# First attention layer of a gated cross-attention model: probabilities made with keys on the partitions, row maxima added in PSUM by selector products

## The chip, the cores and the metric

One core of a Trainium2 chip runs the whole model in one launch. The engines named here are PE (TensorE), DVE (VectorE), ACT (ScalarE), POOL (GpSimd) and SP (SyncE). The metric is the device time of the launch in microseconds.

## What is computed

A batch of 32 sequences of 128 tokens of width 128 goes through four layers, each an attention to a context and a feed-forward part. Only the first attention, A0, is changed:

```python
x = x + tanh(g_xattn[0]) * L0_xattn(layernorm(x), ctx, Wq, bq, Wk, bk, Wv, bv, Wo, bo)
# 16 heads of width 8; the 16 query heads attend to 4 key and value groups
# whose sum enters (the einsums run over g)
# q = x @ Wq + bq, k = ctx @ Wk + bk, v = ctx @ Wv + bv
weight = jnp.einsum('bhtd,bgvd->bhtv', q, k) / math.sqrt(D_HEAD)
weight = jax.nn.softmax(weight, axis=-1)
out = jnp.einsum('bhtv,bgvd->bhtd', weight, v)
out = out.transpose(0, 2, 1, 3).reshape(b, t, N_HIDDEN)
return out @ Wo + bo
```

The kernel sums the four key groups into one key and one value of width 8 that all 16 heads share (`wkvs0`, `bkv0`).

## The kernel before

The kernel has eight stages, one after another: A0, F0, A1, F1, A2, F2, A3, F3. A stage starts when the last residual of the one before has been added. Within a stage the 32 sequences go in eight blocks `c` of four. In A0 two blocks are unrolled in a loop (blocks 1 to 4), the others are written out. Each engine has its own program in a fixed order, and semaphores named `A0_...` join them; so the order that is written is the order that runs.

A block of A0 has 16 rounds `u`. A round handles one unit: one sequence `j` and four of its heads, 128 queries by 4 x 128 keys, one PSUM bank. The fp32 queries and keys are split in three bf16 parts each, so that one bf16 product gives an exact score. The path of a unit before the change:

- PE, line 771: two products, queries on the partitions, into bank 0 or 1.
- DVE, `less_max` (lines 1664 and 1665): row maxima by a reduction, then the scores less the maxima, from PSUM to `ex` in SBUF.
- ACT, line 1241: exponential, SBUF to SBUF.
- PE, line 780: four fp32 transposes into bank 2 or 3, two rounds behind. ACT, line 1239: copy to `pT0`.
- Once per sequence: PE multiplies `v0` by `pT0` (line 794; a column of ones in `v0` gives the sums), ACT copies it, PE transposes it back (806), DVE divides by the sums (1745, 1746), PE transposes (810), ACT copies, PE applies `wo0` (817).
- Once per block: DVE adds the residual (1782, 1783).

Between the rounds lie pieces of the next block, in `SLICES0`: the normalised input is transposed (739), keys and values (743) and queries (747) are projected, POOL splits them into parts (`split`, lines 543 to 551 for keys and 554 to 558 for queries; the call `power` in line 529 is the inverse deviation), and PE transposes the parts (751, 757). All pieces use bank 6, so each waits until ACT has emptied the one before. DVE makes the statistics (1752, 1757, 1645) and the normalised input (1766) of two blocks ahead in `front`.

## Time and profile before

| | us |
|---|---|
| median of 3 runs | 1875.44 (1872.81 to 1878.2) |
| the profiled execution, own time | 1858.33 |
| span in its profile | 1856.5 |
| PE busy | 1383.9 |
| DVE busy | 1350.7 |
| ACT busy | 1006.0 |
| POOL busy | 491.3 |

Busy time is the time in which an engine runs instructions; it says nothing of which wait counts in a stage. The views are read by stage. "PEclk" is the granted clock of TensorE as a share of full speed. In a timeline a row gives start, duration and instruction; instructions in a row overlap at their ends, so the distance between two starts is what one costs.

### The profile page before, as it was taken

How to read it: one execution, taken by the hardware profiler on the slowest of the kernel's cores; microseconds unless marked ns; L12 is line 12 of the kernel's file. 1: busy time of each engine (PE TensorE's matmuls, PEld its weight loads, DVE VectorE, ACT ScalarE, POOL GpSimd, SP SyncE). 2: the span in 40 equal slices, each digit the busy share in tenths (PEclk: the TensorE clock that was granted, in tenths of full speed). 3: DMA queues.
4: the chain of work that ended last, by engine and by line, in shares of the span. 5: the costliest groups of instructions: out<-in, count | busy, mean ns of one | idle time of the engine just before them, and what ended most of it. 6: DMA issues, size and time to landing. Idle time of an engine off the chain costs nothing.

```text
span 1856.5 us, 35646 instructions
## 1 busy us (share of the span) xinstructions
PE 1383.9 (75%) x9716; PEld 1034.4 (56%) x9716; DVE 1350.7 (73%) x4216; ACT 1006.0 (54%) x2812; POOL 491.3 (26%) x499
## 2 busy tenths in 40 slices
PE   3677776987744446677669999999997419999990
PEld 3455553665533334533325666666666319999990
DVE  3888886788879896889955677676767456666657
ACT  3678786342324554410127776777786207777760
POOL 5433530211100000100000022342233335555550
PEclk9899988999865556978879999999999759999995
DMA  7000059400099920100000000000000422222216
GB/s 164 11 7 6 12 79 161 51 0 1 29 133 160 161 34 14 32 1 0 1 0 7 7 23 18 22 30 21 13 22 24 170 91 63 64 67 66 65 52 226
DMA packets 144708, 97.72 MB, mean 53 GB/s; under 512 B 21657, under 2 KB 133933, under 8 KB 143442
## 3 DMA queue, kind: packets, MB, share of 16 engines
q1 hardware_dynamic: 135890, 79.49, 23.2%
q0 software_dynamic: 8704, 16.87, 2.7%
q8 instruction: 53, 0.87, 0.2%
q14 instruction: 61, 0.50, 0.1%
HBM read 42.43 MB, written 54.93 MB: 52 GB/s over the span
## 4 chain that ended last, share of the span: by engine, by line
PE 35%; issue 30%; DVE 19%; ACT 9%; POOL 4%; DMA 1%; DVEq 1%; SPq 0%; ACTq 0%; POOLq 0%
PE bank L1216 6%; PE bank L1208 6%; PE bank L852 5%; ACT att L1362 3%; PE bank L868 3%; PE bank L901 3%; ACT arena L1239 2%; DVE x L2307 2%; PE bank L888 2%; POOL dispatched_rows L628 2%; PE bank L878 2%; DVE nm L1664 2%; PE bank L856 2%; DVE arena L1808 1%; DVE tmp L1942 1%
## 5 line engine op out<-in xcount | busy, mean ns | idle before, releaser
L1239 ACT ACTIVATE arena<-bank 128x512 f32<-128x512 f32 (+6 forms) x440 | 256.2, 614 | 143.2 <-PE bank L1072 62.1
L529 POOL TENSOR_TENSOR rstd<-ve,mhalf 128x4 f32<-128x4 f32 x64 | 67.0, 1046 | 686.9 <-DVE ve L1645 686.9
L1362 ACT ACTIVATE att<-bank,arena 128x128 f32<-128x128 f32 x512 | 181.9, 377 | 80.8 <-DVE arena L1808 79.0
L1582 ACT ACTIVATE att<-bank,arena 128x128 f32<-128x128 f32 x576 | 165.1, 372 | 73.1 <-PE bank L1208 72.9
L628 POOL DMA_INDIRECT dispatched_rows<-arena x128 | 132.9, 1038 | 209.9 <-DVE arena L1726 152.8
L679 POOL DMA_INDIRECT expert_outputs<-arena x144 | 143.4, 996 | 147.5 <-DVE arena L2284 133.7
L1239 ACT ACTIVATE xnT<-bank 128x128 f32<-128x128 f32 (+1 forms) x180 | 63.6, 354 | 188.8 <-PE bank L700 133.6
L1216 PE MATMUL bank<-arena,att 128*128 128x128 f32 x1152 | 154.1, 277 | 1.7 <-ACT att L1582 0.5
L1208 PE MATMUL bank<-xnT,arena 128*128 128x128 f32 x1152 | 154.1, 277 | 0.2 <-ACT xnT L1239 0.2
L1216 PEld LDWEIGHTS bank<-arena,att 128*128 128x128 f32 x1152 | 141.0, 193 | 3.8 <-ACT att L1582 3.8
L1208 PEld LDWEIGHTS bank<-xnT,arena 128*128 128x128 f32 x1152 | 141.8, 194 | 0.6 <-ACT xnT L1239 0.6
L1664 DVE TENSOR_REDUCE nm<-bank 128x4 f32<-128x512 f32 x136 | 93.2, 685 | 54.7 <-PE bank L771 53.2
L1808 DVE TENSOR_REDUCE arena<-bank 128x4 f32<-128x512 f32 x128 | 82.3, 685 | 62.5 <-PE bank L868 60.0
L2270 DVE COPY arena<-arena 128x512 f32 x144 | 61.7, 428 | 83.6 <-issue 83.5
L1241 ACT ACTIVATE att<-att 128x512 f32<-128x512 f32 x144 | 91.1, 632 | 55.8 <-DVE att L1665 49.7
L1362 ACT ACTIVATION_READ_ACCUMULATOR att<-bank,arena 128x1 f32 x512 | 110.6, 216 | 0.0
L1665 DVE TENSOR_TENSOR att<-bank,nm 128x512 f32<-128x512 f32 x136 | 94.0, 691 | 4.7
L1347 ACT ACTIVATE arena<-bank 128x512 f32<-128x512 f32 x128 | 77.7, 607 | 30.5 <-PE bank L852 30.5
L1814 DVE TENSOR_TENSOR att<-att,arena 128x512 f32<-128x512 f32 x128 | 88.7, 693 | 4.4
L868 PEld LDWEIGHTS bank<-arena 64*128 64x128 f32 x1024 | 63.1, 189 | 45.6 <-issue 24.7
L780 PE MATMUL bank<-ident,att 128*128 128x128 f32 x512 | 82.9, 287 | 2.3 <-ACT att L1241 2.1
L868 PE MATMUL bank<-arena 64*128 64x128 f32 x1024 | 75.3, 287 | 12.2 <-ACTq L1354 6.3
(314 smaller groups left out, 3256.7 us busy)
## 6 DMA issues: line engine op xcount, KB each, us to landing
dispatched_rows<-padf SPq DMA_DIRECT2D x16, 2128.5 KB, 35.3
arena<-dispatched_rows SPq DMA_DIRECT2D x144, 64.5 KB
cxT<-in_ctx SPq DMA_DIRECT2D x32, 256.0 KB, 2.9
arena<-in_L_ffn_w SPq DMA_DIRECT2D x8, 1024.0 KB, 13.1
arena<-expert_outputs SPq DMA_DIRECT2D x8, 1024.0 KB, 13.7
expert_outputs<-arena POOLq DMA_INDIRECT x144
dispatched_rows<-arena POOLq DMA_INDIRECT x128
out_x<-x SPq DMA_DIRECT2D x8, 256.0 KB, 3.1
```

The costliest lines, as they stand in the source:

```text
L628: pl.indirect_dma_start(sent, bass.IndirectOffsetOnAxis(di3[:, q:q + 1], 0), rows3[:, q, :], None)\
L679: pl.indirect_dma_start(sent_out, bass.IndirectOffsetOnAxis(xtu3[:, s, P:P + 1], 0), yt3[:, s, :], None, bounds_check=TOP3 * TOKENS - 1, o ...
L852: last = nc.tensor.matmul(A[:, :], wqk3[:, t, pair * P:pair * P + P], cxT[:, p, :] if t else xnT[:, :], start=True, stop=True)
L868: last = nc.tensor.matmul(bank[side][:, i * P:i * P + P], q, k, start=True, stop=True)
L1208: last = nc.tensor.matmul(bank[s % 2][:, k * P:k * P + P], w1c3[:, s % 4, k * P:k * P + P], xnT[:, (s % 4) * P:(s % 4) * P + P], start=Tru ...
L1216: last = nc.tensor.matmul(bank[2 + s % 2][:, 0:P], h3[:, s % 2, k * P:k * P + P], w2c3[:, s % 4, k * P:k * P + P], start=(k == 0), stop=(k ...
L1239: copy = lambda o, i: nc.scalar.activation(o, i, ACT.Copy)
L1362: last = nc.scalar.activation(ex3_of(w, side)[:, i, :], bank[side][:, i * P:i * P + P], ACT.Exp, bias=nm3[:, w % 2, h:h + 1], accum_out=su ...
L1582: last = nc.scalar.activation(h3[:, s % 2, k * P:k * P + P], bank[s % 2][:, k * P:k * P + P], ACT.Gelu, bias=b1c3[:, s % 4, k:k + 1])
L1664: step(v.tensor_reduce(nm[:, slot, :], src, AX, ALU.max))
L1665: v.tensor_tensor(dst, src, nm[:, slot, :].unsqueeze(2).to_broadcast([P, CB, P]), ALU.subtract)\
L1808: v.tensor_reduce(nm3[:, w % 2, side:2 * HQ:2], b4(side), AX, ALU.max, negate=True).then_inc(sem("A3_max"), 1)
```

## The change

A unit's probabilities are now made with keys on the partitions, so that they need no transposing. The product of line 771 stays, but only for the row maxima: DVE reduces them, negated, into `nm0` (`maxima`). After the four units of a sequence, DVE splits the 16 maxima per query into three bf16 parts (`parts_of_maxima`, a copy and three subtractions of 16 or 32 elements a partition, all within SBUF). PE transposes these (`maxima_T`), ACT copies them to `mT0`. Six rounds behind the first product, `scores_T` writes a unit again with keys on the partitions: four selector products (`sel0_`, a constant matrix that picks the three parts of one head and spreads them over 128 keys) put the negated maxima in the bank, and one product of 512 columns adds the scores. ACT takes the exponential straight from PSUM into `pT0`. The subtraction, the four transposes and the copy are gone. The value product follows ten rounds behind, and the later steps 12 to 14, so the drain at the end has 12 rounds and not 8.

The four heads of a unit of `scores_T` are every other head, so `Wo`'s rows are laid out in that order ahead of the launch. The pieces run up to two blocks ahead: projections and POOL's `split` of block c + 2 and the transposes of the split parts of block c + 1 lie in block c. POOL builds `sel0_` in the beginning, and adds the value bias in `values0`. The `front` of block c + 3 lies in rounds 0, 1, 2, 6 and 8. The context loads and the first fills of `dispatched_rows` on SP's queue hang on the projections, and so move up by a block. Eight semaphores of the last stage are replaced by ones that are free by then.

```diff
+EARLY0 = [(0, s) for s in range(3)] + [(1, s) for s in range(3)] + [(0, s) for s in range(3, 8)]
...
+def slices0_at(u, c):
+    at = ({4: (1, 3), 5: (1, 4), 6: (1, 5), 7: (1, 6), 8: (1, 7), 9: (2, 0), 10: (2, 1), 11: (2, 2)} if isinstance(c, int) and c == 0 else
+          {1: (2, 0), 2: (2, 1), 3: (2, 2), 7: (1, 3), 8: (1, 4), 10: (1, 5), 12: (1, 6), 14: (1, 7)})
+    last = c if isinstance(c, int) else 0
...
+            step(pl.memset(nmp0[:, :, :, PARTS_M:P // 2], 0.0))
+            step(pl.memset(of_head0[:, :], 0.0))
+            for r in range(2):
+                for x_ in range(3):
+                    step(pl.affine_select(out=of_head0[:, :], in_=of_head0[:, :], compare_op=ALU.not_equal, fill=1.0, base=-(r * (P // 2) + x_ * HEADS),
+                                          pattern=[[-1, HEADS]], channel_multiplier=1))
...
+            pl.tensor_copy(sel0_[:, :, :], of_head0[:, :].unsqueeze(2).to_broadcast([P, HEADS, P])).then_inc(sem("A0_selectors"), 1)
...
+            def split(c, p, ahead):
...
+                if ahead:
+                    power("A0", c + 1)
                 pl.wait_ge(sem("A0_raw"), c * 2 + 2)
...
+                if free is not None:
+                    pl.wait_ge(sem("A0_pv"), free)
+                raw = kvraw0[:, p, :].rearrange("p (j d) -> p j d", j=CB)
+                pl.tensor_tensor(v0[:, p, :, 0:D0], raw[:, :, D0:KV0], bkv0[:, D0:KV0].unsqueeze(1).to_broadcast([P, CB, D0]), ALU.add)\
+                    .then_inc(sem("A0_values"), 1)
...
+                    split(c + 2, 1 - p, True)
+                    values0(c + 1, p, c * CB)
...
+                def maxima_T(c, j):
+                    pe.wait_ge(sem("A0_parts"), c * CB + (j + 1))
+                    reach(pe, "A0_mT", c, CB, j)
+                    if j == 2:
+                        reach(pe, "x_done", c, 1, 1)
+                    nc.tensor.transpose(mT_at, nmp0[:, j % 2, :, :].rearrange("p r a -> p (r a)"), ident16[:, :]).then_inc(sem("A0_mT_full"), 1)
+                def scores_T(c, p, k):
+                    j, g = divmod(k % UNITS, QUARTERS)
+                    gh, a = divmod(g, 2)
+                    rows = slice(P // 2 * a, P // 2 * a + P // 2)
+                    of_m = slice(P // 2 * a, P // 2 * a + PARTS_M)
+                    reach(pe, "A0_exp", c, UNITS, k - 1)
+                    if g == 0:
+                        pe.wait_ge(sem("A0_mT"), c * CB + (k // QUARTERS + 1))
+                    for i in range(HQ):
+                        nc.tensor.matmul(bank[2 + a][:, i * P:i * P + P], sel0_[of_m, 2 * (HQ * gh + i) + a, :], mT0[of_m, j % 2, :],
+                                         start=(i == 0), stop=False, skip_group_check=True)
+                    last = nc.tensor.matmul(bank[2 + a][:, :], kT0[rows, p, j, a * P:a * P + P], qT0[rows, p, j, gh * W:gh * W + W],
+                                            start=False, stop=True, skip_group_check=True)
+                    last.then_inc(sem("A0_scores_T"), 1)
+                def values(c, p, j):
+                    pe.wait_ge(sem("A0_exp"), c * UNITS + (QUARTERS * j + QUARTERS))
+                    reach(pe, "A0_outT", c, CB, j)
+                    if j % CB == 0:
+                        pe.wait_ge(sem("A0_values"), c + (j // CB + 1))
+                    for g in range(QUARTERS):
+                        rows0 = slice(ROWS0 * g, ROWS0 * g + ROWS0)
+                        last = nc.tensor.matmul(bank[4][rows0, :], v0[:, p, j % CB, :], pT0[:, j % 2 * QUARTERS + g, :], start=True, stop=True)
+                    last.then_inc(sem("A0_pv"), 1)
...
+                        if u % QUARTERS == 1 and due(5):
+                            maxima_T(c, (u - 5) // QUARTERS)
+                        if due(6):
+                            scores_T(c, old(u, 6), u - 6)
+                        if u % QUARTERS == 2 and due(10):
+                            values(c, old(u, 10), (u - 10) // QUARTERS)
...
-                                last = nc.tensor.transpose(bank[2 + v % 2][:, i * P:i * P + P], ex[:, v % 4, i, :], ident[:, :])
-                            last.then_inc(sem("A0_pT_full"), 1)
...
+                        if u % QUARTERS == 0 and due(12):
+                            j = (u - 12) // QUARTERS
+                            pe.wait_ge(sem("A0_outT"), c * CB + (j + 1))
+                            reach(pe, "A0_oT", c, CB, j)
...
+                                last = nc.tensor.transpose(bank[5][:, i * P:i * P + P], outT0[:, i * P:i * P + P], ident[:, :])
+                            last.then_inc(sem("A0_out"), 1)
...
+                        for n, ahead, s in (slices0_at(u, c) if live else []):
+                            pe.wait_ge(sem("A0_slice_gone"), c * 8 + (len(EARLY0) + n))
+                            piece(c + ahead, (p + ahead) % 2, s, 6)
...
-                            copy(pT0[:, v % PT0, :, :], b4(2 + v % 2)).then_inc(sem("A0_pT"), 1)
...
-                            exp(ex[:, u % 4, :, :], ex[:, u % 4, :, :]).then_inc(sem("A0_exp"), 1)
...
+                        if due(6):
+                            k = u - 6
+                            act.wait_ge(sem("A0_scores_T"), c * UNITS + (k + 1))
+                            if k % QUARTERS == 0:
+                                reach(act, "A0_pv", c, CB, k // QUARTERS - 1)
+                            exp(pT0[:, k % PT0, :], bank[2 + k % 2][:, :]).then_inc(sem("A0_exp"), 1)
+                        if u % QUARTERS == 1 and due(5):
+                            j = (u - 5) // QUARTERS
+                            act.wait_ge(sem("A0_mT_full"), c * CB + (j + 1))
+                            copy(mT0[:, j % 2, :], mT_at).then_inc(sem("A0_mT"), 1)
+                        if u % QUARTERS == 3 and due(11):
+                            j = (u - 11) // QUARTERS
+                            act.wait_ge(sem("A0_pv"), c * CB + (j + 1))
+                            reach(act, "A0_out", c, CB, j)
+                            copy(outT0[:, :], bank[4][:, :]).then_inc(sem("A0_outT"), 1)
...
-                    less_max(b4(u % 2), ex[:, u % 4, :, :], u % 2, "A0")
...
+                def maxima(c, u):
                     j, qd = divmod(u, QUARTERS)
-                    if qd != 0:
-                        return
-                    dve.wait_ge(sem("A0_oT_full"), c * (2 * CB) + (2 * j + 1))
-                    o = bank[4 + j % 2][:, :].rearrange("p (i q r) -> p q i r", i=HQ, r=ROWS0)
-                    sums0 = rs[:, :].rearrange("p (q i a) -> p q i a", q=QUARTERS, a=1)
+                    dve.wait_ge(sem("A0_scores"), c * UNITS + (u + 1))
+                    v.tensor_reduce(nm0[:, j % 2, HQ * qd:HQ * qd + HQ], b4(u % 2), AX, ALU.max, negate=True).then_inc(sem("A0_max"), 1)
+                def parts_of_maxima(c, j):
+                    reach(dve, "A0_mT_full", c, CB, j - 1)
+                    dve.sem_inc(s_held, 1)
+                    dve.wait_ge(sem("A0_max"), c * UNITS + (QUARTERS * j + QUARTERS))
+                    dve.sem_inc(s_held, 1)
+                    m, twice = nm0[:, j % 2, :], nm0[:, j % 2, :].unsqueeze(1).to_broadcast([P, 2, HEADS])
+                    first, second, third = (nmp0[:, j % 2, :, x_ * HEADS:x_ * HEADS + HEADS] for x_ in range(3))
+                    step(v.tensor_copy(first, twice))
+                    v.tensor_tensor(second, twice, first, ALU.subtract)
+                    step(v.tensor_tensor(rest0[:, :], m, first[:, 0, :], ALU.subtract))
+                    v.tensor_tensor(third, rest0[:, :].unsqueeze(1).to_broadcast([P, 2, HEADS]), second, ALU.subtract).then_inc(sem("A0_parts"), 1)
...
+                            maxima(c, u)
+                        if live and u % QUARTERS == QUARTERS - 1:
+                            parts_of_maxima(c, u // QUARTERS)
+                        if u % QUARTERS == 0 and due(12):
+                            normal(c, (u - 12) // QUARTERS)
...
+                        if live and not first and ahead and u in (0, 1, 2, 6, 8):
+                            front(c + 3, (0, 1, 2, 6, 8).index(u))
```

Two places in the order of instructions. First DVE in block 0, of the change: `maxima` is line 1786, `parts_of_maxima` lines 1796 to 1799.

```order
L1827 TENSOR_SCALAR xn<-x,mv,rstd 128x128 [waits A0_xnT,inverse_deviation]
L1827 TENSOR_SCALAR xn<-x,mv,rstd 128x128
L1786 TENSOR_REDUCE arena<-bank1 128x4 [waits A0_scores]
L1796 CAST arena<-arena 128x2x16 [waits A0_max]
L1797 TENSOR_TENSOR arena<-arena 128x2x16 [waits vector_steps]
L1798 TENSOR_TENSOR arena<-arena 128x16
L1799 TENSOR_TENSOR arena<-arena 128x2x16 [waits vector_steps]
```

The same engine and block before:

```order
L1664 TENSOR_REDUCE nm<-bank1 128x4 [waits A0_pT_full,A0_scores]
L1665 TENSOR_TENSOR att<-bank1,nm 128x512 [waits vector_steps]
L1664 TENSOR_REDUCE nm<-bank0 128x4 [waits A0_pT_full,A0_scores]
L1665 TENSOR_TENSOR att<-bank0,nm 128x512 [waits vector_steps]
L1745 RECIPROCAL rs<-bank5 128x16 [waits A0_oT_full]
```

The subtraction after each reduction (128x512) is gone, and after every fourth reduction stand four small instructions whose operands all lie in SBUF.

Second PE in block 0, around round 9, of the change: line 797 is the first product, 807 `maxima_T`, 819 the selectors, 821 the second product, 769 a piece.

```order
L797 MATMUL bank1<-arena 128x256 [waits A0_max]
L797 MATMUL bank1<-arena 128x256
L807 MATMUL bank7<-ident16,arena 128x128 [waits A0_mT,A0_parts]
L819 MATMUL bank3<-arena 128x128 [waits A0_exp]
L819 MATMUL bank3<-arena 128x128 x3
L821 MATMUL bank3<-arena 128x512
L769 MATMUL bank6<-ident,xn 128x128 [waits normalised,A0_slice_gone]
L769 MATMUL bank6<-ident,xn 128x128 x3
```

The same engine and block before:

```order
L771 MATMUL bank1<-arena 128x256 [waits A0_less_max]
L771 MATMUL bank1<-arena 128x256
L780 MATMUL bank3<-ident,att 128x128 [waits A0_pT,A0_exp]
L780 MATMUL bank3<-ident,att 128x128 x3
L757 MATMUL bank6<-ident16,arena 128x128 [waits A0_split,A0_slice_gone]
L757 MATMUL bank6<-ident16,arena 128x128 x7
```

Each round's four transposes have become four selectors and a product, and one round in four PE waits in `maxima_T` for DVE's small instructions with everything else behind it.

## Rows read from the trace of the kernel before

**Rows 1.** The page, busy time of each engine over the span

```profile
PE 1383.9 (75%) x9716; PEld 1034.4 (56%) x9716; DVE 1350.7 (73%) x4216; ACT 1006.0 (54%) x2812; POOL 491.3 (26%) x499
```

**Rows 2.** Busy time by stretch: blocks 2 to 4, 6, 7, drain

```profile
110.20:215.30 105.10, 79.66 (x638) 56.17 (x637) 87.48 (x166) 80.12 (x147) 43.27 (x39) 0.94 0.03 8
250.20:281.60 31.40, 25.93 (x214) 18.37 (x213) 25.21 (x43) 26.71 (x49) 13.44 (x12) 0.95 0.95 134
281.60:308.00 26.40, 19.23 (x149) 12.68 (x146) 23.68 (x42) 19.78 (x39) 0.00 (x0) 1.00 1.31 160
308.00:316.60 8.60, 4.88 (x30) 2.69 (x30) 3.14 (x7) 3.33 (x8) 0.00 (x0) 0.89 1.30 158
```

**Rows 3.** Groups of instructions with their idle time, blocks 2 to 4

```profile
L1664 DVE TENSOR_REDUCE nm<-bank 128x4 f32<-128x512 f32 x49 | 33.6, 685 | 15.7 <-PE bank L771 15.7
L1665 DVE TENSOR_TENSOR att<-bank,nm 128x512 f32<-128x512 f32 x48 | 33.2, 691 | 1.6
...
L1241 ACT ACTIVATE att<-att 128x512 f32<-128x512 f32 x48 | 30.4, 633 | 18.5 <-DVE att L1665 15.5 <-ACT arena L1239 1.1 <-ACT xnT L1239 0.6
L1239 ACT ACTIVATE arena<-bank 128x1024 bf16<-128x1024 bf16 x12 | 12.5, 1045 | 0.1
...
L1645 DVE TENSOR_SCALAR ve<-mv 128x4 f32<-128x4 f32 x3 | 7.9, 2643 | 0.1
...
L1239 ACT ACTIVATE arena<-bank 128x128 f32<-128x128 f32 x12 | 3.3, 273 | 0.0
```

**Rows 4.** Timeline of POOL and DVE in block 2: start, duration, instruction

```profile
123.68 1.16 POOL L556 TENSOR_TENSOR arena<-arena 128x512 f32<-128x512 f32 x1
124.81 3.55 POOL L557 TENSOR_TENSOR arena<-arena 128x1536 bf16<-128x1536 f32 x1
128.44 2.12 POOL L558 TENSOR_TENSOR arena<-arena 128x1024 bf16<-128x1024 f32 x1
125.75 2.64 DVE L1645 TENSOR_SCALAR ve<-mv 128x4 f32<-128x4 f32 x1
```

**Rows 5.** Timeline of POOL and DVE in stage F0

```profile
365.90 2.49 POOL L585 TENSOR_TENSOR arena<-arena 128x512 f32<-128x512 f32 x2
366.52 0.68 DVE L1907 CAST arena<-arena 128x32 f32<-128x32 uint32 x1
367.24 1.43 DVE L1909 TENSOR_TENSOR arena<-iota,arena 128x32 f32<-128x32 f32 x2
```

**Rows 6.** Timeline of PE in block 2

```profile
138.41 0.62 PE L757 MATMUL bank<-ident,arena 128*128 128x128 bf16 x8 [0.64 <-ACT arena L1239]
138.87 0.28 PE L810 MATMUL bank<-ident,arena 128*128 128x128 f32 x1
138.98 0.38 PE L771 MATMUL bank<-arena 128*128 128x256 bf16 x2
139.20 0.60 PE L780 MATMUL bank<-ident,att 128*128 128x128 f32 x4
...
140.88 1.06 PE L794 MATMUL bank<-arena 128*32 128x512 f32 x8
141.88 0.49 PE L817 MATMUL bank<-wo,arena 128*128 128x128 f32 x2
```

**Rows 7.** Timeline of ACT in block 2: two evictions of 512

```profile
143.09 1.07 ACT L1239 ACTIVATE arena<-bank 128x512 f32<-128x512 f32 x2
```

**Rows 8.** A stretch behind DVE's wait, with the granted clock third from the end

```profile
131.00:132.00 1.00, 1.00 (x9) 0.67 (x11) 1.00 (x2) 0.44 (x1) 0.53 (x1) 0.50 0.00 0
```

**Rows 9.** Timeline of POOL in the beginning

```profile
18.32 0.26 POOL L547 CAST arena<-arena 128x96 bf16<-128x96 f32 x1 [0.17 <-POOL arena L544]
...
19.80 0.40 POOL L551 COPY arena<-arena 128x256 bf16<-128x256 bf16 x1 [0.19 <-POOL arena L550]
20.16 1.26 POOL L554 TENSOR_TENSOR arena<-arena,bq 128x512 f32<-128x512 f32 x1
21.38 3.44 POOL L555 TENSOR_TENSOR arena<-arena,bq 128x1536 bf16<-128x1536 f32 x1
```

More of the change, by code:

```diff
@@ L552, in split @@
+                if ahead:
+                    power("A0", c + 1)
                 pl.wait_ge(sem("A0_raw"), c * 2 + 2)
[L553 to L556 removed]
+                raw = qraw0[:, p, :].rearrange("p (h d) -> p h d", d=D0)
@@ L557, in split @@
+                first, second, third = qs[:, :, 0:3, :], qs[:, :, 3:6, :], qs[:, :, 6:8, :]
+                pl.tensor_tensor(q0[:, :, :], raw, bq0[:, :, :], ALU.add)
+                step(pl.tensor_tensor(first, of(raw, first), of(bq0[:, :, :], first), ALU.add))
+                pl.tensor_tensor(qrest0[:, :, :], q0[:, :, :], qs[:, :, 0, :], ALU.subtract)
                 step(pl.tensor_tensor(second, of(q0[:, :, :], second), first, ALU.subtract))
                 pl.tensor_tensor(third, of(qrest0[:, :, :], third), second[:, :, 0:2, :], ALU.subtract).then_inc(sem("A0_split"), 1)
-                if more:
-                    power("A0", c + 1)
@@ L563, in _ @@
+            values0(1, 1, None)
+            power("A0", 2)
+            split(2, 0, True)
             step.loop(2 * 6)
-            with pl.Fori(0, NC // 2 - 1) as i:
+            with pl.Fori(0, NC // 2 - 2) as i:
                 step.turn(i)
                 for p in range(2):
-                    split(i * 2 + (p + 1), 1 - p, True)
-            step.end(NC // 2 - 1)
+                    c = i * 2 + (p + 1)
+                    split(c + 2, 1 - p, True)
+                    values0(c + 1, p, c * CB)
@@ L824, in heads0 @@
+                body(0, 0, first=True)
                 setup()
@@ L1318, in heads0 @@
-                act.sem_inc(sem("A0_slice_gone"), 1)
-                act.sem_inc(sem("A0_pT"), CRED)
-                act.sem_inc(sem("A0_exp"), CRED)
-                act.sem_inc(sem("A0_pv_batch"), 2)
-                act.sem_inc(sem("A0_oT"), 3)
-                for s in range(kA):
-                    piece(0, 0, s, first=True)
-                body(0, 0, True, True)
+                            last = copy(kT0[half, p, :, q * P:q * P + P], A16[half, 0:W].rearrange("p (j t) -> p j t", j=CB))
@@ new lines, in piece, with body @@
+                        last.then_inc(gone, 1)
+                    else:
+                        copy(qT0[:, p, s - 4, :], A16[:, :]).then_inc(gone, 1)
+                        if s == 7:
+                            act.wait_ge(gone, n + 1)
+                            act.sem_inc(sem("A0_slices_ready"), 1)
+                def body(c, p, first=False, live=True):
+                    for u in range(UNITS if live else DRAIN0):
+                        due = lambda lag: (live and u >= lag) or (not first and u < lag)
+                        if due(6):
[13 more added lines that the diff above has]
+                            copy(outT0[:, :], bank[4][:, :]).then_inc(sem("A0_outT"), 1)
+                        if u % QUARTERS == 1 and due(13):
+                            j = (u - 13) // QUARTERS
+                            act.wait_ge(sem("A0_oT_full"), c * CB + (j + 1))
+                            reach(act, "A0_y", c, CB, j - 1)
+                            copy(oT0[:, j % 2, :], bank[5][:, 0:P]).then_inc(sem("A0_oT"), 1)
+                        for n, ahead, s in (slices0_at(u, c) if live else []):
+                            piece(c + ahead, (p + ahead) % 2, s, c * 8 + (len(EARLY0) + n), 6)
@@ L1326, in heads0 @@
+                for n, (c, s) in enumerate(EARLY0):
+                    piece(c, c, s, n, (6 - n) % 8)
+                body(0, 0, first=True)
                 setup()
@@ L2330 @@
     laid["L3_ffn_w2"] = _np.transpose(_np.reshape(inputs["L3_ffn_w2"], (E3, P, K3, P)), (3, 0, 2, 1)).reshape(P, E3, H3)
+    laid["L0_xattn_Wo"] = _np.reshape(_np.transpose(_np.reshape(inputs["L0_xattn_Wo"], (2, HQ, 2, D0, P)), (0, 2, 1, 3, 4)), (P, P))
     for name, value in laid.items():
```

285 lines of the change are left out of this document (120 added, 165 removed).

## The prediction

> **What bounds the kernel now.** I read the page first: no engine fills the span, PE is busy 75% of it and DVE 73% [rows 1], so the change has to be judged in its own stage. The windows by stretch give that stage. Blocks 2 to 4 take 105.1 us, 35.0 each, of which DVE is busy 87.5 (83%), ACT 80.1, PE 79.7 and POOL 43.3; block 6 takes 31.4, block 7 26.4 and the drain 8.6, so A0 ends at 316.6 of 1856.5 [rows 2].
>
> The groups with their idle time tell who waits. The reduction and the subtraction take 0.685 and 0.691 us per unit, 22 of DVE's 29.2 us a block; DVE idles 15.7 us in three blocks for line 771, which waits for `less_max` two units back; and ACT idles 15.5 us for DVE [rows 3]. DVE sets the pace, with PE a short way behind.
>
> One more row matters. `ve`, a TENSOR_SCALAR of 4 elements a partition, takes 2.64 us every time [rows 3]. The timeline shows why: it starts at 125.75 and ends at 128.39, just when POOL's line 557 ends (124.81 + 3.55 = 128.36) [rows 4]. In F0 the same is seen twice in a row: a cast of 32 elements takes 0.68 and ends near the end of the first of two POOL instructions, and of the two comparisons behind it (two operands in SBUF) the pair takes 1.43 and ends 0.28 after the second POOL instruction (365.90 + 2.49 = 368.39) [rows 5]. So a small DVE instruction with its operands in SBUF waits for the POOL instruction under way, and the next DVE instruction can wait for the next.
>
> **The change, part by part, for one block of 16 rounds.**
>
> DVE. Minus 16 subtractions of 0.691: 11.1 us. Plus 4 x `parts_of_maxima`. From the comparisons, once their 1.21 of waiting is off, one such instruction costs some 0.2 [rows 5]: 4 x 4 x 0.2 = 3.2. `ve` moves to round 2, where POOL is idle: minus 2.5. So 29.2 - 11.1 + 3.2 - 2.5 = 18.8 us: DVE stops being the bound.
>
> PE. The transposes cost 4 x 0.11 = 0.44 a round (line 810, one such, starts 0.11 ahead of line 771) [rows 6]. Selectors and product are not in the trace. Nearest are line 757, 8 bf16 products of 128 columns in 0.46, so 0.057 each, and line 771, two of 256 in 0.22, so 0.11 each, 0.22 for 512 [rows 6]: 4 x 0.057 + 0.22 = 0.45. Bounds: 0.22, if the selectors hide under the product, and 0.66, if each selector costs 0.11, as an fp32 transpose or a 256-column product does. I take 0.45, since both rows are bf16 and of these shapes, so PE gains nothing; the ends would move a block by -3.7 and +3.4 us. Its whole block, added up from the same starts: first products 3.5, second 7.2, `maxima_T` 0.2, values 4 x 1.0, fp32 transposes back 4 x 0.55, `wo0` 4 x 0.32 [rows 6], pieces 4.3 (0.45 input, two projections of eight passes at 0.11, 0.9 each, 0.25 and 4 x 0.46 the parts): 22.7 us with rounding.
>
> ACT. The exponential (0.63) and the copy (0.6) become one instruction: it drops some 8 us, from 26.7 (80.1 / 3) to 19, and is no bound.
>
> So no engine needs more than 22.7 us; then the waits count. I followed PE through a block:
>
> - `mT0`: `scores_T` of a sequence's first unit needs a copy on ACT that stands behind the exponential of the `scores_T` just issued. PE's tail of 0.16 (0.27 long, 0.11 apart), some 0.1 for semaphores, ACT 0.5 per 512 columns (two in 1.07) [rows 7] and the copy 0.27 [rows 3] are 1.0 us, against some 0.34 of other work on PE. The four sequences lose 0.3, 0.7, 0.9 and 0.9, more where a 1.05 eviction of 1024 columns [rows 3] lies in front: 2.8 us.
> - The transposes back wait in the same way for `outT0`: exponential, then a copy of 0.6, 1.35 us against at least 0.66 of work: 0, 0.5, 1.0 and 1.0, 2.5 us. Bank 6 after the key parts costs another 0.6.
> - Sum 5.9, so 28.6 us at full clock.
> - `parts_of_maxima` and POOL. POOL's `split` begins when the raw keys are out, at the end of round 2; 2.5 us for the keys, 1.0 `power`, then 11.6 for the queries in five instructions (1.27, 3.46, 1.16, 3.1, 2.1) [rows 4, 9]; line 557 is 3.55 long where DVE was ahead of it. Measured from PE's round 3, the queries run from 3.7 to 15.2. `parts_of_maxima` of sequence 1 is due in round 7, at 7.0. Its copy waits for the end of the 3.46 instruction (8.5), the next one for that of 1.16 (9.8), the last for that of 3.1 (13.2). PE wants the result in round 9, at 9.8, with everything behind it, the second products and so ACT. That is 3.5 us, if DVE's third instruction, with no wait ahead of it, slips in behind its neighbour; it is 5.8 if it loses too. I take 3.5, since it is issued back to back. The bound below is nothing, if DVE wins.
> - The clock. Behind today's wait for `ve` PE runs at half clock, granted 0.50 [rows 8], for some 3 us; that costs about 1.5 a block, and the new gap is as long. 1.5.
>
> Sum: 28.6 + 3.5 + 1.5 = 33.6 us, against 35.0.
>
> A rule bears on `parts_of_maxima`. The Trainium skill, "SBUF — State Buffer", section "Who interferes with whom", says that DVE and GpSimd share one port pair under an exclusive lock: a copy or tensor_scalar in a 2-port mode takes it, and a tensor_tensor with both inputs in SBUF contends with GpSimd instructions that read SBUF, while a tensor_reduce never does. By that rule, the trace agrees (2.64 for `ve`), all four new instructions are exposed, and the removed subtraction, with its input in PSUM, never was. Without the rule the sum would be 30 or less a block.
>
> Edges. POOL builds `sel0_` ahead of the first split: 2048 elements. By the slope from 96 to 256 elements (0.26, 0.40) some 2.0 us, by line 555 (3.44 for 1536) 4.6 [rows 9]; I take 2.0, since it has one operand as those two. The memset and six selections ahead of it fit in POOL's idle time. In block 0 POOL splits block 1's queries beside `parts_of_maxima` of sequence 0 and block 2's beside sequence 3 and `setup`, and PE cannot go on past round 5 without either: some 4 us each, which the shorter rounds give back. Blocks 0 and 1 together: 0, with an end of -8 and +8.
>
> Blocks 2 to 5: 4 x (33.6 - 35.0) = -5.6. Block 6, no split of POOL's left: 28.6 - 31.4 = -2.8. Block 7, without pieces: 22.7 - 4.3 + 5.2 = 23.6, -2.8. Drain, from the last maxima on, one after another: parts and their copy 1.5, four second products with their exponentials 0.8 each and 0.6, values 1.0, copy 0.7, transposes 0.6, division 0.7, transpose and copy 0.6, `wo0` 0.4, residual 1.5, semaphores 0.7: 11.5, against 8.6 [rows 2], +2.9. The last projections, and with them the first fills on SP's queue, come a block earlier; F0's pace does not hang on them: 0. The swapped semaphores of the last stage: 0. Sum -8.3.
>
> The profiled execution took 1858.33, 17 us less than the median of 1875.44; the difference is carried to the median: 1867.
>
> **The rivals.**
>
> POOL costs little. DVE gets the port whenever it asks, or PE's slack hides it: 29 us a block, no gap and no half clock. 5 x (29 - 35) - 2.7 = -32.7: 1843. For it: DVE's work is only 18.8. Against it: `ve` and the cast waited to the end, each time. 0.22.
>
> The port decides against the change. DVE loses at each of the four instructions and at the two TENSOR_SCALARs of `xn` in round 6, so that the parts come only when POOL's queries are done (5.8), and rounds 8 to 10 wait for a late DVE too: 28.6 + 5.8 + 1.5 + 1.1 = 37. 5 x 2 - 2.7 + 1 = +8: 1884. It decides from 36.7 us a block on. The selectors at their upper bound would do the same alone. For it: two losses in a row [rows 5]; against it: PE has some slack in rounds 8 to 10. 0.22.
>
> The wait only changes its name: stall and saving cancel, 34.5 to 35.5 a block, 1872 to 1876. 0.16.
>
> **How the numbers follow.** The forecast has 0.40; its own range, 32.5 to 34.4 us a block, is 1861 to 1871. 0.3% is 5.6 us, about what a measurement of this kernel can tell from no change: below 1869.8 is faster, above 1881.1 slower. Faster: 0.22 + 0.32 of the forecast's 0.40 = 0.54. Slower: 0.21 of the second rival's 0.22. Same: 0.16 + 0.08 + 0.01 = 0.25. The range goes from 1840, most of the first rival, to 1884, the second.
>
> **What the profile after would show.** Line 1786 (`maxima`) keeps 0.685 and the subtraction is gone. Lines 1796 to 1799 take 0.2 each in three sequences of a block and 1 to 3 us in the second, ending with POOL's instructions. PE idles most for line 1799, ahead of 807. A block takes 33 to 34 us. If 819 and 821 take more than 0.5 a round, the PE term is wrong; if 1796 to 1799 never exceed 0.3, the first rival is right; if block 7 takes more than 24, the hand-offs were put too low.

## The result: 1.6% slower

The changed kernel takes 1902.76 us in the median of 4 runs (1900.78 to 1913.39), the kernel before 1875.35 beside it; the ratio is 1.0158, with a 95% interval of 1.0128 to 1.0189. The forecast was 1867, the range 1840 to 1884. In a second comparison on another chip (label `c_after`, below) the ratio is 1.0194 (1.0156 to 1.0231).

The busy times of the page of the changed kernel, against [rows 1]:

```profile
PE 1424.3 (75%) x9876; PEld 1023.7 (54%) x9876; DVE 1320.8 (70%) x4216; ACT 945.6 (50%) x2716; POOL 495.0 (26%) x508
```

DVE and ACT have less to do, as the change intended, PE more. The two spans differ by 43 us (1856.5 and 1899.5), the medians by 27. Where A0 ends tells them apart. It ends at 316.5 before and at 341.5 now, 25.0 later. What lies behind A0 took 1540.0 and 1558.0 us; for the same kernel before it took 1568.3 in its second trace, on a chip on which that kernel's median is 1883, and 1536 to 1539 in four experiments on a chip where it is 1858. So this remainder goes mostly with the chip, and the 25 us are A0's. By blocks, from first product to first product (line 771 before, 797 now):

| stretch | before | now | forecast of the difference | measured |
|---|---|---|---|---|
| to the first product | 36.4 | 37.6 | +2.0, within the next row | +1.2 |
| blocks 0 and 1 | 73.2 | 86.6 | 0 (-8 to +8) | +13.4 |
| blocks 2 to 5 | 140.0 | 147.7 | -5.6 | +7.7 |
| block 6 | 31.4 | 28.6 | -2.8 | -2.8 |
| block 7, to its last product | 25.8 | 25.1 | -2.8 | -0.6 |
| drain, from there to the end of A0 | 9.8 | 15.8 | +2.9 | +6.0 |

Of the 13.4 us of the first two blocks 10.9 are block 0's (34.1 before, 45.0 now).

The windows of the changed kernel's trace, as in [rows 2]. The first is three blocks long, from round 2 of block 2 on; the second one block, from round 2 of block 6 on. Then come rounds 2 to 15 of block 7, the drain, and three short stretches for the clock; the first of these, at 1.00, holds no reading of the clock (last section):

```profile
core 0: us, PE busy (x) PEld busy (x) DVE busy (x) ACT busy (x) POOL busy (x), PEclk, DMA share, GB/s
127.40:239.70 112.30, 91.30 (x698) 49.55 (x696) 79.99 (x164) 57.14 (x112) 42.23 (x39) 0.86 0.03 7
274.60:303.20 28.60, 24.79 (x214) 12.97 (x213) 16.49 (x43) 17.44 (x35) 0.25 (x1) 1.00 1.34 157
303.20:325.70 22.50, 19.24 (x151) 9.09 (x150) 13.56 (x34) 10.77 (x25) 0.00 (x0) 1.00 1.28 163
325.70:341.50 15.80, 9.64 (x77) 4.56 (x74) 4.44 (x13) 6.32 (x14) 0.00 (x0) 0.99 0.10 14
48.00:56.00 8.00, 8.00 (x53) 4.90 (x51) 5.38 (x17) 5.48 (x7) 1.02 (x1) 1.00 0.00 1
146.00:152.00 6.00, 5.88 (x30) 2.57 (x30) 2.60 (x7) 1.53 (x4) 0.00 (x0) 0.50 0.00 0
156.00:162.00 6.00, 5.09 (x44) 2.37 (x43) 3.60 (x10) 3.84 (x7) 0.00 (x0) 1.00 0.02 3
```

A block in the middle takes 37.4 us where 33.6 were forecast and 35.0 stood before, with PE's clock down to 0.86 in the mean. Block 6, in which POOL has almost nothing to do, takes 28.6 at full clock. The waits of PE in the first window say what stands between the two (reading: who waited, for whom, in total, times, longest):

```profile
PE bank L807 <- DVE arena L1799: 12.8, 3, 4.3
PE bank L819 <- ACT arena L1296: 2.0, 6, 0.5
PE bank L855 <- ACT arena L1296: 1.8, 6, 0.4
```

Once in each block PE waits 4.3 us for the last of the four instructions that split the maxima. The timeline of DVE at that place in block 2, its rounds 6 to 8:

```profile
135.78 4.53 DVE L1827 TENSOR_SCALAR xn<-x,mv,rstd 128x128 f32 x2
140.23 0.68 DVE L1786 TENSOR_REDUCE arena<-bank 128x4 f32<-128x512 f32 x1
141.06 2.25 DVE L1796 CAST arena<-arena 128x32 bf16<-128x32 f32 x1 [0.15 <-DVE arena L1786]
143.34 0.19 DVE L1797 TENSOR_TENSOR arena<-arena 128x32 bf16<-128x32 f32 x1
143.45 2.09 DVE L1798 TENSOR_TENSOR arena<-arena 128x16 f32<-128x16 f32 x1
145.58 0.19 DVE L1799 TENSOR_TENSOR arena<-arena 128x32 bf16<-128x32 f32 x1
145.69 0.68 DVE L1786 TENSOR_REDUCE arena<-bank 128x4 f32<-128x512 f32 x1
```

and of POOL beside it:

```profile
135.53 3.47 POOL L575 TENSOR_TENSOR arena<-arena,bq 128x1536 bf16<-128x1536 f32 x1
139.07 1.16 POOL L576 TENSOR_TENSOR arena<-arena 128x512 f32<-128x512 f32 x1
140.19 3.08 POOL L577 TENSOR_TENSOR arena<-arena 128x1536 bf16<-128x1536 f32 x1
143.35 2.16 POOL L578 TENSOR_TENSOR arena<-arena 128x1024 bf16<-128x1024 f32 x1
```

Each DVE instruction that takes 2 us or more in place of 0.2 ends with one of POOL's: line 1796 at 143.31, POOL's 577 at 143.27; line 1798 at 145.54, POOL's 578 at 145.51. The next one (1797) takes its normal 0.19, and the one behind that (1798) loses again, to the POOL instruction that has begun meanwhile. The reductions (1786), which read PSUM, take 0.68 whatever POOL does. That agrees with the rule that the prediction cited from the Trainium skill, "SBUF — State Buffer", section "Who interferes with whom".

PE, which needs these parts in its own round 9:

```profile
141.16 0.38 PE L797 MATMUL bank<-arena 128*128 128x256 bf16 x2
145.83 0.29 PE L807 MATMUL bank<-ident,arena 128*128 128x128 bf16 x1 [4.29 <-DVE arena L1799]
146.05 0.61 PE L819 MATMUL bank<-arena 48*128 48x128 bf16 x4
146.45 0.63 PE L821 MATMUL bank<-arena 64*128 64x512 bf16 x1
147.01 0.47 PE L860 MATMUL bank<-ident,arena 128*128 128x128 f32 x1
147.28 0.63 PE L797 MATMUL bank<-arena 128*128 128x256 bf16 x2
...
154.21 0.38 PE L821 MATMUL bank<-arena 64*128 64x512 bf16 x1
```

Behind the idle 4.29 us the same products take 0.63 in place of 0.38: the lower of the two levels, 1.2 GHz, as the granted 0.50 of the window from 146 on says, until about 153.5.

The kernel before has a wait of this kind too. Behind DVE's line 1645, the `ve` of [rows 4], its PE idles once in each middle block:

```profile
130.25 0.34 PE L810 MATMUL bank<-ident,arena 128*128 128x128 f32 x1 [4.66 <-DVE arena L1746]
```

So the change did not bring in the wait for POOL; it moved it, from `ve` to the parts. The half clock behind it lasts 3.4 us there (130.4 to 133.9) and 10.2 here (143.2 to 153.4).

### The profile page after: what moved, and what is told of

The parts are those of the page before. It is cut to its first block, busy times and chain, and to the rows that moved or that the text cites. A ratio compares the mean times of both kernels' runs of the same rounds, so it can differ in the third digit from the quotient of the medians.

```text
span 1899.5 us, 35674 instructions
## 1 busy us (share of the span) xinstructions
PE 1424.3 (75%) x9876; PEld 1023.7 (54%) x9876; DVE 1320.8 (70%) x4216; ACT 945.6 (50%) x2716; POOL 495.0 (26%) x508
## 4 chain that ended last, share of the span: by engine, by line
PE 40%; issue 29%; DVE 18%; ACT 8%; POOL 2%; another core or an unknown queue 1%; DMA 1%; SPq 1%; DVEq 1%; ACTq 0%; POOLq 0%
PE bank L1265 6%; PE bank L1273 6%; PE bank L909 5%; PE bank L958 3%; PE bank L925 3%; ACT att L1415 2%; PE bank L945 2%; ACT arena L1296 2%; DVE x L2376 2%; PE bank L833 2%; PE bank L935 2%; PE bank L819 2%; PE bank L913 2%; PE bank L821 1%
## 5 line engine op out<-in xcount | busy, mean ns | idle before, releaser
L1296 ACT ACTIVATE arena<-bank 128x512 f32<-128x512 f32 (+7 forms) x344 | 195.5, 589 | 170.8 <-PE bank L1129 61.6
L1786 DVE TENSOR_REDUCE arena<-bank 128x4 f32<-128x512 f32 x128 | 87.6, 687 | 93.8 <-PE bank L797 90.2
L1298 ACT ACTIVATE arena<-bank 128x512 f32<-128x512 f32 x128 | 76.6, 598 | 102.3 <-PE bank L821 101.0
L1876 DVE TENSOR_REDUCE arena<-bank 128x4 f32<-128x512 f32 x128 | 82.3, 684 | 63.0 <-PE bank L925 58.3
L1400 ACT ACTIVATE arena<-bank 128x512 f32<-128x512 f32 x128 | 77.6, 607 | 38.7 <-PE bank L909 38.1
L958 PE MATMUL bank<-wo,arena 128*128 128x128 f32 x512 | 72.8, 301 | 27.5 <-DVE arena L1890 21.8
L958 PEld LDWEIGHTS bank<-wo,arena 128*128 128x128 f32 x512 | 66.7, 211 | 32.9 <-DVE arena L1890 19.6
```

The costliest lines, as they stand in the source:

```text
L958: last = nc.tensor.matmul(bank[7][:, j * P:j * P + P], oT3[:, j % 2, k, :], wo3[:, k, :], start=(k == 0), stop=(k == 7))
L1296: copy = lambda o, i: nc.scalar.activation(o, i, ACT.Copy)
L1786: v.tensor_reduce(nm0[:, j % 2, HQ * qd:HQ * qd + HQ], b4(u % 2), AX, ALU.max, negate=True).then_inc(sem("A0_max"), 1)
```

## Experiments

Times on different chips differ by more than the effects (the kernel before has a median of 1857.7 to 1883.1), so each kernel is compared with the kernel before on its own chip, and read by where block 2 begins (its first product), by a block's length (mean of blocks 2 to 4) and by where A0 ends:

| label | block 2 begins | a block | A0 ends | ratio to before (95%) |
|---|---|---|---|---|
| before | 109.6 | 35.0 | 316.5 | 1 |
| `c_before` | 111.7 | 35.3 | 317.8 | 1.0004 (0.9984 to 1.0024) |
| after | 124.2 | 37.4 | 341.5 | 1.0158 (1.0128 to 1.0189) |
| `c_after` | 126.0 | 37.4 | 352.3 | 1.0194 (1.0156 to 1.0231) |
| `e1_no_query_split` | 117.0 | 30.4 | 312.5 | 0.9963 (0.9948 to 0.9979) |
| `e2_short_instructions` | 122.2 | 31.5 | 317.5 | 1.0002 (0.9979 to 1.0024) |
| `e3_split_waits` | 116.2 | 30.7 | 315.0 | 0.9991 (0.9971 to 1.0012) |
| `e4_no_selectors` | 117.1 | 36.2 | 324.6 | 1.0060 (1.0043 to 1.0077) |
| `e5_pe_busy` | 125.1 | 34.8 | 345.6 | 1.0234 (1.0203 to 1.0264) |
| `e6_no_parts` | 113.2 | 30.7 | 309.1 | 0.9955 (0.9932 to 0.9978) |
| `e7_first_block` | 120.3 | 30.7 | 313.4 | 1.0016 (0.9998 to 1.0035) |
| `e8_split_waits_setup` | 116.4 | 30.7 | 314.6 | 0.9977 (0.9959 to 0.9995) |
| `e8_again` | 116.4 | 30.7 | 314.7 | 0.9972 (0.9955 to 0.9988) |
| `e9_busy_first_block` | 111.3 | 30.7 | 304.3 | 0.9946 (0.9929 to 0.9963) |

The expectations below count the rounds of PE from another place. What they call the beginning of block 2 is the product of its round 2 (119.7 for e8, where the first product is at 116.4), while their 109.6 and 111.7 of the kernel before are first products. Their blocks 0 and 1 of 50.9 and 38.9 us are 45.0 and 41.6, and the wait that they put in round 7, where DVE makes the parts, stands in PE's round 9.

The ends of A0 hold one more thing: the drain takes 15.8 us in the first trace of the changed kernel and 16.6 to 22.1 in the others, for the same steps, as the clock stays up in it or falls.

The theory after the result: DVE's small instructions in SBUF lose against POOL's split, PE idles behind them and then runs at half clock, in the middle blocks and, more, in the first. The rival: PE's own work, the selectors and the second product, costs more than forecast, and the waits only hide it.

**The split left out.**

```diff
+                if not isinstance(c, int) or c > 1:
+                    one = slice(0, 1)
+                    step(pl.tensor_tensor(q0[:, one, :], raw[:, one, :], bq0[:, one, :], ALU.add))
...
+                    return
                 pl.tensor_tensor(q0[:, :, :], raw, bq0[:, :, :], ALU.add)
```

> The changed kernel with POOL's split of the queries left out from block 2 on: in place of its five instructions POOL adds one head three times (three instructions of under 0.3 us), so the queries' bf16 parts of blocks 2 to 7 are stale. Port theory (DVE's small instructions with operands in SBUF wait for POOL's instruction under way, PE idles behind them and then runs at half clock): blocks 1 to 5, now 38.9, 37.6, 37.3, 37.4 and 34.9 us, fall to the 28.6 us that block 6 takes without a split, 43 us in all, and block 0 gives back some 5; A0 ends near 293 in place of 341, and the time is near 1855. Rival (PE's own work: selectors and second product take 0.53 us a round, and what DVE loses is hidden behind it): blocks of 36 us and more, time 1890 or above.

A block takes 30.4 us, at full clock (the window is three blocks long, from round 1 of block 2 on):

```profile
118.70:209.80 91.10, 81.01 (x698) 45.58 (x696) 57.29 (x165) 56.70 (x111) 11.04 (x33) 1.00 0.03 9
```

So POOL's 11.2 us of query instructions cost PE 7.0 us a block. The block expected, 28.6, was too short; block 6 has no input pieces, and these have. The end of A0 expected, 293, was missed by 19 us (312.5): the short blocks are 2 to 5 alone. Block 1 still takes 42.6, at half clock up to 104.6, and the drain is 4.7 longer than in the changed kernel.

**The split in shorter instructions.** Each of the five query instructions in a loop over the four sequences.

```diff
-                step(pl.tensor_tensor(second, of(q0[:, :, :], second), first, ALU.subtract))
+                for j in range(CB):
+                    h = slice(j * HEADS, (j + 1) * HEADS)
+                    last = pl.tensor_tensor(second[:, h], of(q0[:, h, :], second[:, h]), first[:, h], ALU.subtract)
+                step(last)
```

> The changed kernel with each of POOL's five query instructions cut in four, one of 16 heads each: same work, instructions of 0.3 to 0.9 us. If DVE gets its turn at the end of the POOL instruction under way, its waits shrink with them: the two subtractions of xn from 4.5 to 1.5 us at most, the four parts of the maxima in sequence 1 from 4.7 to 2.5 at most, a block takes 32 to 34 us and the time is near 1880. If DVE has to wait for a gap in POOL's stream, or if the port is not what holds it, nothing changes: 37.4 us a block, 1900. If POOL pays more than 0.1 us for each extra instruction the split is longer, up to 14 us, and more of DVE's instructions meet it.

DVE in round 7 of block 2:

```profile
136.75 0.26 DVE L1809 CAST arena<-arena 128x32 bf16<-128x32 f32 x1 [0.15 <-DVE arena L1799]
137.04 0.93 DVE L1810 TENSOR_TENSOR arena<-arena 128x32 bf16<-128x32 f32 x1
137.90 0.16 DVE L1811 TENSOR_TENSOR arena<-arena 128x16 f32<-128x16 f32 x1
138.09 0.38 DVE L1812 TENSOR_TENSOR arena<-arena 128x32 bf16<-128x32 f32 x1
```

The four take 1.7 us in place of 4.7, and a block 31.5. So DVE gets its turn at the end of one POOL instruction, and the wait is as long as what is left of it. The first product comes 2.1 us later (39.7), since the longer split (POOL's 1536 elements take 3.87 in four pieces, 3.47 in one) lies on the path at the start.

**The split waits for the parts.**

```diff
+                if behind is not None:
+                    pl.wait_ge(sem("A0_parts"), behind)
                 pl.tensor_tensor(qrest0[:, :, :], q0[:, :, :], qs[:, :, 0, :], ALU.subtract)
...
-            split(1, 1, False)
+            split(1, 1, False, 1)
...
-            split(2, 0, True)
+            split(2, 0, True, CB)
...
-                    split(c + 2, 1 - p, True)
+                    split(c + 2, 1 - p, True, c * CB + 2)
```

> The changed kernel with POOL's last three query instructions of each split held back until DVE has issued the parts of the maxima of sequence 1 (in block 0: of sequence 0 for block 1's split, of sequence 3 for block 2's). Port theory: lines 1796 to 1799 take 0.2 us each in all sequences and PE's wait of 4.3 us for line 1799 is gone, with its half clock; xn in round 6 still meets the 3.5 us instruction and costs up to 3 us. A block takes 30 to 33 us, block 0 loses 8 of its 50.9 us, and the time is near 1865. Rival (PE's own work): no change beyond 2 us a block, 1890 or above.

Nothing is left out here, and it takes 26.5 us off A0 (341.5 to 315.0): 8.0 off blocks 0 and 1, 25.4 off blocks 2 to 5, less 7 for block 7 and its drain, where the clock falls at 291.5. DVE in rounds 6 to 8 of block 2:

```profile
127.80 3.54 DVE L1829 TENSOR_SCALAR xn<-x,mv,rstd 128x128 f32 x2
131.26 0.68 DVE L1788 TENSOR_REDUCE arena<-bank 128x4 f32<-128x512 f32 x1
132.09 0.18 DVE L1798 CAST arena<-arena 128x32 bf16<-128x32 f32 x1 [0.15 <-DVE arena L1788]
132.31 0.19 DVE L1799 TENSOR_TENSOR arena<-arena 128x32 bf16<-128x32 f32 x1
132.42 0.17 DVE L1800 TENSOR_TENSOR arena<-arena 128x16 f32<-128x16 f32 x1
132.62 0.19 DVE L1801 TENSOR_TENSOR arena<-arena 128x32 bf16<-128x32 f32 x1
...
133.82 3.38 DVE L1829 TENSOR_SCALAR xn<-x,mv,rstd 128x128 f32 x2
```

Both pairs of `xn` still lose 3 us to POOL, and the block is only 0.3 above that of `e1_no_query_split`: it matters which DVE instruction waits, not how many. In block 0 the gate gives 1.4 us and not the 8 expected: PE needs block 1's queries in round 5, and holding POOL back moves the round behind it from 47.7 to 49.4. Block 1 gives the other 6.6.

**No selectors.**

```diff
-                    for i in range(HQ):
-                        nc.tensor.matmul(bank[2 + a][:, i * P:i * P + P], sel0_[of_m, 2 * (HQ * gh + i) + a, :], mT0[of_m, j % 2, :],
-                                         start=(i == 0), stop=False, skip_group_check=True)
```

> The changed kernel with the four selector products of each second score product left out: the exponentials are taken of scores without their maxima. The parts, their transposition and all waits stay. Port theory: PE saves 0.22 us a round, 3.5 us a block, where it is not waiting anyway, but the gap of 4.3 us in round 7 stays, so that a block takes 34 to 36 us and the time is 1880 to 1890. Rival (PE's own work sets the blocks): at half clock and in the hand-offs the four products cost twice that and more, a block falls to 31 or less, and the time is 1865 or below.

A block falls by 1.2 us, to 36.2, and block 6 by 1.9, to 26.7; PE waits longer instead:

```profile
PE bank L807 <- DVE arena L1796: 15.4, 3, 5.1
```

So the selectors cost 0.12 us a round where nothing waits, and the rival is out as the main cause of the long blocks.

**PE kept busy in the gap.**

```diff
+                    if j == 1:
+                        reach(pe, "A0_mT", c, CB, j)
+                        for _ in range(72):
+                            nc.tensor.transpose(mT_at, ident16[:, :], ident16[:, :])
                     pe.wait_ge(sem("A0_parts"), c * CB + (j + 1))
```

> The changed kernel with 72 bf16 transposes of the identity, into the place in PSUM that the maxima's transposition writes afterwards, ahead of PE's wait for the parts of sequence 1 in every block: some 4 us of idle PE are filled, nothing else changes. If the half clock behind the gap (7.7 us of it in each of blocks 1 to 4) is due to the gap, PE keeps its full clock and a block falls from 37.4 by 3 to 4 us, the time by 15 to 18. If the clock falls for another reason, or the rounds behind the gap wait for DVE and ACT anyway, a block stays above 36.5 and the time within 5 us of the changed kernel's.

```profile
142.29 4.18 PE L806 MATMUL bank<-ident 128*128 128x128 bf16 x72
146.76 0.23 PE L811 MATMUL bank<-ident,arena 128*128 128x128 bf16 x1 [0.29 <-DVE arena L1803]
146.92 0.39 PE L823 MATMUL bank<-arena 48*128 48x128 bf16 x4
147.16 0.38 PE L825 MATMUL bank<-arena 64*128 64x512 bf16 x1
```

The clock stays up (0.38 behind the gap) and a block takes 34.8, a little less gain than the 3 to 4 us expected: 2.6 of the 7.0 us are the clock's, the other 4.4 the stall itself. The whole kernel got no faster: blocks 6 and 7 have no gap, and the fillers cost them 4 us each; the drain, which has no fillers, takes 20.5, at half clock. That part of the expectation was a miss.

**The parts left out.**

```diff
-                    step(v.tensor_copy(first, twice))
-                    v.tensor_tensor(second, twice, first, ALU.subtract)
...
+                    dve.sem_inc(sem("A0_parts"), 1)
```

> The changed kernel with the four instructions that split the maxima left out: DVE only signals, and the selectors add zeros. The subtractions of xn still meet POOL's 3.5 us instruction in round 6. If it is the parts that stop PE, blocks 2 to 4 take 29 to 31 us, as in e3, and PE's wait of 4.3 us in round 7 is gone; if xn's wait is enough to stop PE, 33 us or more.

30.7 us a block, although `xn` takes 4.41 in round 6. Blocks 0 and 1 take 74.4 us in place of 86.6: 12.2 of the 13.4 that they lost hang on the parts too.

**The first block.** A new layout of its pieces, which did not work:

```diff
-    at = ({4: (1, 3), 5: (1, 4), 6: (1, 5), 7: (1, 6), 8: (1, 7), 9: (2, 0), 10: (2, 1), 11: (2, 2)} if isinstance(c, int) and c == 0 else
+    at = ({6: (1, 3), 8: (1, 4), 9: (1, 5), 10: (1, 6), 11: (1, 7), 12: (2, 0), 13: (2, 1), 14: (2, 2)} if isinstance(c, int) and c == 0 else
...
-            split(2, 0, True, CB)
+            power("A0", 3)
+            split(2, 0, False, CB + 1, UNITS + 1)
```

> The kernel of e3 (POOL's last three query instructions behind the parts of the maxima) with a first block laid out anew: block 1's key and query pieces in rounds 6 and 8 to 11 in place of 4 to 8, block 2's input pieces in rounds 12 to 14 in place of 9 to 11, and POOL's query split for block 2 behind the first maxima of block 1, so that it doesn't meet the setup on DVE. Theory for the first block (PE waits 6.3 us for POOL's split of block 1's queries and 9.3 us at the end for DVE's setup, which meets POOL's split): A0 ends 8 to 12 us earlier than in e3, at 303 to 307, and the time is 8 to 12 us under e3's, below that of the kernel before. Rival (those waits only hide PE's own extra pieces, six more in the first block): within 3 us of e3.

Block 2 begins at 120.3, 4 us later than in e3, and A0 ends at 313.4 where 303 to 307 were expected: the setup is free of POOL, but the split for block 2 now ends in block 1, the one for block 3 starts late and meets `xn` there (4.68 us, of which PE idles 4.2). A0 ends 1.6 earlier than in e3 all the same: the drain takes 17.0, against 22.1 there, where the clock falls at 291.5 and not at 306.3. Then two gates alone:

```diff
-            split(1, 1, False, 1)
+            split(1, 1, False)
...
-            split(2, 0, True, CB)
+            split(2, 0, True, UNITS + 1, "A0_max")
```

> The kernel of e3 with two gates set otherwise in the first block: POOL's split of block 1's queries isn't held back at all (PE waits for it in round 4), and the last three query instructions for block 2 wait for the first maxima of block 1, which come behind the setup on DVE, in place of the parts of sequence 3. Blocks 2 to 7 as in e3. In e3 the setup's instructions lost 4.8 us to POOL (1.5, 2.9 and 1.0 us in place of 0.6, 0.2 and 0.2), with PE idle, and round 4 began 1.8 us later than without the gate. Port theory: A0 ends 6 to 8 us earlier than in e3 (315, or 308 with its drain at full clock), and the time is 0.2 to 0.6% under that of the kernel before. Rival (POOL's held instructions now meet ve and the parts in rounds 2 and 3 of block 1, and the wait only moves): within 2 us of e3, level with the kernel before.

The setup shrinks as expected (PE's longest wait there 4.9 in place of 9.3), yet block 2 begins at 116.4, as in e3 (116.2): PE runs at half clock until round 9 of block 1 (102.8). The rival's sum was right. Last, the idle PE of the first block filled:

```diff
+                    if n == 7:
+                        busy(bank[7][:, 0:P // 2].bitcast(BF16), 80)
...
+                    if isinstance(c, int) and c == 0 and j == 0:
+                        busy(mT_at, 50)
...
+                busy(bank[6][:, 0:P // 2].bitcast(BF16), 60)
```

> The kernel of e8 with idle PE filled in the first block alone: transposes of the identity into places in PSUM that are overwritten next, 80 ahead of the first query piece of block 0, 50 ahead of the wait for the parts of sequence 0 and 60 ahead of the setup. In e8 PE runs at half clock in rounds 0 to 7 of block 0 and from the setup to round 7 of block 1, some 17 us and 25 us. If the clock is what the early gaps cost beyond their own length, block 2 begins at 110 to 113 in place of 119.7 (before: 109.6 and 111.7), A0 ends 6 to 10 us earlier than in e8, and the time is 0.5 to 0.8% under that of the kernel before. If the gaps alone cost, or fillers at half clock outlast them, block 2 begins at 118 or later and the time is e8's.

> The kernel of e8 again, on the chip of e9, for the comparison of the two: block 2 begins at 119.7 within 1 us in any theory, and the time is 0.2% under that of the kernel before.

The windows of `e8_again`, then of `e9_busy_first_block`:

```profile
49.00:56.00 7.00, 6.97 (x47) 4.29 (x46) 4.42 (x14) 4.83 (x6) 0.24 (x1) 1.00 0.00 0
72.00:88.00 16.00, 13.96 (x63) 8.36 (x64) 9.84 (x33) 3.65 (x9) 7.60 (x8) 0.50 0.01 2
89.00:97.00 8.00, 7.88 (x37) 3.30 (x36) 3.04 (x7) 2.73 (x6) 5.32 (x3) 0.50 0.01 2
```

```profile
49.00:56.00 7.00, 5.90 (x64) 3.37 (x61) 5.98 (x22) 6.14 (x10) 0.39 (x1) 1.00 0.00 0
72.00:88.00 16.00, 15.22 (x71) 9.03 (x69) 9.54 (x29) 4.74 (x10) 9.55 (x11) 0.50 0.06 18
89.00:97.00 8.00, 6.96 (x64) 3.72 (x62) 6.62 (x15) 4.61 (x10) 5.18 (x3) 1.00 0.00 1
```

The 1.00 of `e8_again` from 49 to 56 holds no reading of the clock ahead of 55.2, and its products take 0.63 there; in `e9_busy_first_block` the reading is real, and they take 0.38. Block 2 begins at 111.3, 5.1 earlier, less than the 7 to 10 expected, because the clock falls behind the setup all the same (0.50 from 72 to 88) and only recovers sooner. Still, blocks 0 and 1 now take 73.9 us, level with the kernel before (73.2 and 75.2 in its two traces). Block 7 and the drain also keep their clock longer, which gives 5 us more. With 0.9946 (0.9929 to 0.9963) this version beats both kernels. What the same gate on POOL would give the kernel before, whose PE waits 4.66 us in a block too, was not tried; so no run shows that the new layout itself is what gains.

The controls, `c_after` and `c_before`:

> The changed kernel again, unchanged, as the measure for the experiments run on the same chip. Both theories: A0 ends at 341.5 within 1 us, blocks of 37.4 us; the time is that of the kernel before plus 25 to 29 us.

> The kernel before again, unchanged, for a second trace of it. Both theories: A0 ends at 316.5 within 1 us. The first trace's span is 17 us under the median of its runs; if that came from a stage behind A0, this trace shows where.

Neither keeps within the 1 us expected. `c_before` ends A0 1.3 us later than the first trace. `c_after` ends it 10.8 later: 1.8 of it by block 2, 2.2 in block 5, and 7.0 in the drain, which takes 26.5 us from the last residual but one and not 19.5, at half clock. The trace of the changed kernel shown above was one in which the drain kept its clock.

## Why the prediction was wrong

- **What bounds the kernel.** Right: DVE was the bound, and it stops being one (80.0 of 112.3 us).
- **Where the miss lies.** The sum was -8.3 and A0 measured +24.9. Of these 33.2 us, 14.6 lie in the beginning, 13.3 in blocks 2 to 5 (3.3 a block), and 5.3 in block 7 and the drain.
- **Blocks 0 and 1: 0, within 8.** This step failed: +13.4, over half of the loss. The waits were named ("some 4 us each"), and PE's 4.5 us in round 5 came as said, but the words "which the shorter rounds give back" did not hold. In block 0 PE's pair of products takes 0.6 us from the first round to round 12 (65.7), where the kernel before has 0.38 again from 42.3 on. Then DVE's setup is late by what the parts and `xn` lost, PE idles 7.7 us there (2.5 before), and runs at half clock into block 1. The two gates of `e8_split_waits_setup` take 7.9 us off the two blocks (86.6 to 78.7), filling PE's gaps another 4.9 (73.9). That is the whole loss, within what the two traces of the kernel before differ by (73.2, 75.2).
- **The port wait, 3.5 a block.** The mechanism was right in place, instruction and releaser. The size was not: the third instruction loses too, which was the alternative of 5.8, of which PE feels 4.4. The choice "since it is issued back to back" was wrong by the rows: the one issued back to back is the one that loses.
- **The clock, 1.5 a block.** 2.6 by `e5_pe_busy`. It was taken from the 3 us at half clock behind the gap of the kernel before; behind the new one PE works 7 us so.
- **PE, 0.45 a round for selectors and product.** 0.53: 0.22 from line 819 to 821 and 0.31 from there to the next, 1.3 us in 16 rounds. That is past the 0.5 that the prediction set as the sign of a wrong PE term. A block without port waits takes 30.4, not 28.6. These 1.8, with 0.9 more for the port and 1.1 for the clock, make the 37.4 in place of 33.6.
- **Block 6, 28.6.** Met exactly, for the wrong reason: the sum counted input pieces that block 6 no longer has (2.3 us) and was short by as much in product and hand-offs. Block 7 gained 0.6 us and not 2.8; its 25.1 is past the 24 that the prediction set as the sign that the hand-offs were put too low. The drain cost 6.0 more than before and not 2.9.
- **`sel0_`, +2.0.** 1.90 on POOL, +1.2 for the first product.
- **The rivals.** The second was the right one for a block (37 forecast, 37.4 measured); its 1884 was too low, mostly because it took about nothing for the first two blocks and for block 7 and the drain, which lost 13.4 and 5.4.

The sum with the measured terms: 1.2 + 13.4 + 7.7 - 2.8 - 0.6 + 6.0 = 24.9, where the medians differ by 27.4. The drain's share goes by the trace: in `c_after`, the same kernel, the drain takes 22.1.

## What to carry to other kernels

When work is moved from large DVE instructions that read PSUM to small ones within SBUF, look at what POOL runs at that moment and who waits for them: four instructions of 0.2 us cost 7.0 us a block here, and one wait on a semaphore in POOL's program gave 6.7 back. Place POOL's long instructions behind the small ones that PE waits for, and let those that nobody waits for soon (`xn` here) meet them. Work out the first pass of a pipeline by itself; its lags and its setup have less cover than the middle, and one gap in PE is paid twice, by its length and by the clock behind it. Look for the same wait in the kernel before as well: what the gates give back is a gain of the new layout only if the old one has no such gate to win.
